# The small MLP's steps moved into the last slots of clustered attention, and the first batch's inputs taken ahead of the others

## The reference

```python
def first_block(z):                              # z = _layernorm(x) without weights
    u = _layernorm(z, ln1_g, ln1_b)
    q, k, v = (einsum('bsd,dhf->bshf', u, W) for W in (Wq, Wk, Wv))
    qb = softmax(einsum('bshf,hfn->bshn', q, Whq))      # cluster shares, 32 per head
    kb = softmax(einsum('bshf,hfn->bshn', k, Whk))
    logits = einsum('bqhf,bkhf->bhqk', q, k) / sqrt(DH) + 0.1 * einsum('bqhn,bkhn->bhqk', qb, kb)
    z = einsum('bshf,hfd->bsd', softmax(logits) @ v, Wo) + z           # clustered attention
    y = relu(_layernorm(z, ln2_g, ln2_b) @ W1 + b1) @ W2 + b2          # the small MLP, 512 wide
    return z + y
x = x + first_block(_layernorm(x))
x = x + two_local_layers(_layernorm(x))    # attention in windows of 64 tokens, and a gated MLP, twice
```

## Time and profile before

| | |
|---|---|
| median of 3 runs | 1464.22 us (1463.91 to 1464.61) |
| profiled execution, its own time | 1465.65 us |
| span of the profile | 1463.8 us |
| mean granted clock of PE | 0.962 |
| busy, share of the span | PE 87%, DVE 75%, ACT 68%, POOL 56% |
| instructions | 27861 |

### The profile page before, as it was taken

The page is one execution under the profiler, slowest core; times in us unless marked ns, Lnnn a source line. Parts: engine busy times, 40 slices in busy tenths (PEclk is TensorE's granted clock), DMA queues, the critical chain, the costliest instruction groups (busy, mean ns, idle before and its releaser), DMA issues.

```text
span 1463.8 us, 27861 instructions
## 1 busy us (share of the span) xinstructions
PE 1268.3 (87%) x9636; PEld 643.2 (44%) x9636; DVE 1090.7 (75%) x1943; ACT 998.3 (68%) x2313; POOL 822.2 (56%) x1005
## 2 busy tenths in 40 slices
PE   3378989998998988679589999998988999999898
PEld 1112222222222322157256666665534666666554
DVE  4778888888888877223489999995447999999644
ACT  4236766676666666577488999985337999999632
POOL 3666666667766640022577888870028888877200
PEclk9659999999999999989799999999999999999999
DMA  3523333343334330010111111110101111111001
GB/s 103 110 42 65 73 59 65 60 79 58 66 58 73 65 59 1 1 57 1 37 26 27 27 30 27 28 27 2 47 15 42 31 30 27 27 27 31 1 17 41
DMA packets 161120, 60.87 MB, mean 42 GB/s; under 512 B 139691, under 2 KB 152789, under 8 KB 160981
## 3 DMA queue, kind: packets, MB, share of 16 engines
q1 hardware_dynamic: 160980, 59.09, 19.1%
HBM read 8.60 MB, written 2.10 MB: 7 GB/s over the span
## 4 chain that ended last, share of the span: by engine, by line
PE 29%; ACT 11%; DVE 7%; issue 4%; POOL 2%; ACTq 0%; DVEq 0%; POOLq 0%
ACT la_s L1735 8%; PE la_ring L1360 6%; PE la_ring L1372 3%; PE la_s L1393 3%; PE la_pT L1467 3%; DVE la_prob L1624 2%; PE la_pT L1406 2%; PE la_m L1539 2%; PE la_ring L1455 1%; PE la_pT L1457 1%; PE la_s L1455 1%; PE la_s L1457 1%; ACT la_v_own L1777 1%; PE la_s L1385 1%; PE la_o L1422 1%
## 5 line engine op out<-in xcount | busy, mean ns | idle before, releaser
L618 DVE TENSOR_REDUCE row_max<-max_ps 128x2 f32<-128x1024 f32 x256 | 312.9, 1222 | 70.6 <-PE max_ps L430 69.2
L670 ACT ACTIVATE prob<-scores_ps 128x1024 f32<-128x1024 f32 x256 | 262.2, 1024 | 147.8 <-PE scores_ps L410 144.3
L1735 ACT ACTIVATE la_s<-la_s,la_bias,la_inv 128x128 f32<-128x128 f32 x512 | 223.4, 442 | 7.0 <-DVE la_bias L1612 7.0
L1886 POOL TENSOR_TENSOR la_turned<-la_raw,lw_rot 128x1024 f32<-128x1024 f32 x64 | 150.9, 2358 | 115.6 <-PE la_ring L1372 70.1
L1360 PE MATMUL la_ring<-lw_wqkv,la_hT 128*128 128x512 f32 x384 | 202.4, 638 | 15.3 <-DVE la_swapped L1587 6.7
L410 PE MATMUL scores_ps<-stack 128*128 128x512 f16 x512 | 155.7, 386 | 42.0 <-ACT prob L670 41.1
L1892 POOL TENSOR_TENSOR la_turned<-la_turned,la_swapped 128x1024 f32<-128x1024 f32 x64 | 150.7, 2355 | 5.0
L444 PE MATMUL heads_ps<-prob,v_pad 128*32 128x512 f32 x1024 | 137.2, 608 | 1.1 <-ACT prob L670 1.1
L430 PE MATMUL max_ps<-stack 24*128 24x512 f16 x512 | 102.5, 397 | 31.2 <-DVE row_max L618 18.5
L410 PEld LDWEIGHTS scores_ps<-stack 128*128 128x128 f16 x512 | 34.2, 97 | 208.7 <-ACT prob L670 161.3
L1587 DVE TENSOR_TENSOR la_swapped<-la_ring,lw_rot 128x256 f32<-128x256 f32 x256 | 90.8, 415 | 33.3 <-ACT la_raw L1746 23.8
(11 more groups left out here) (177 smaller groups left out, 2765.7 us busy)
## 6 DMA issues: line engine op xcount, KB each, us to landing
la_v_back<-la_v_own SPq DMA_DIRECT2D x112, 128.0 KB, 2.3
X<-in_x SPq DMA_DIRECT2D x8, 256.0 KB, 5.4
stack<-stack_tok SPq DMA_TRANSPOSE x128, 3.2
out<-X SPq DMA_DIRECT2D x8, 256.0 KB, 2.3
lw_wqkv<-in_wqkv SPq DMA_DIRECT2D x2, 768.0 KB, 4.8
stack<-shift_row SPq DMA_DIRECT2D x64, 2.0 KB
lw_rot<-in_rot SPq DMA_DIRECT2D x2, 512.0 KB, 6.5
lw_w<-in_fw SPq DMA_DIRECT2D x2, 341.0 KB
```

Of the source, the lines that this page charges most:

```text
L618: nc.vector.tensor_reduce(row_max[:, grp % 2, w // 2, :, w % 2], max_ps[:], AX.X, ALU.max).then_inc(max_made, 1)
L670: nc.scalar.activation(prob[:, c % 4, 2 * pr:2 * pr + 2, :], scores_ps[:], ACT.Exp, scale=1.0 / LOGIT_SCALE).then_inc(exp_made, 1)
L1735: ins = nc.scalar.activation(s_ps[:, place(h), :], s_ps[:, place(h), :], ACT.Exp, bias=bias[:, T % 2, h:h + 1], scale=inv[:, T % 4, h:h + ...
L1886: nc.gpsimd.tensor_tensor(spun, raw[:, T % 2].rearrange("p s (h f) -> p s h f", f=LD), rot[:, T % TPB, :, 0, :].unsqueeze(2).to_broadcast( ...
```

## The change

It has two parts. **The opening:** SP loads batch 0, the four arrays that the fold of the cluster weights needs, and six more that the first tile needs, ahead of the other seven batches; each group has its own semaphore. The statistics and scales are made for batch 0 first (`FIRST`), those of batches 1 to 3 behind it, and those of batches 4 to 7 on DVE right behind the cluster subtraction of tile 0. The scales of the other 28 tiles (`REST`) are made within tile 1's steps. For the first four tiles ACT, not POOL, scales the input and writes both leading parts (`leading_part`); DVE only writes the query's rest. `standardise` starts 24 slots later. **The small MLP:** `mlp_and_turn` is gone. Its steps stand in the slots of attention from slot 239 on, seven slots to a batch (`mlp_at`), and each engine does them after the rest of the slot. Its buffers lie in the half of `stack` that is free by then, its PSUM tiles in banks that attention no longer uses. Square root and reciprocal are replaced by an addition and a power on POOL. The input side of its layer norm is made as each batch is finished: DVE's four aggregates behind the statistics in slot `41 + 32b`, POOL's `invert_input` in slot `42 + 32b`, DVE's `input_shift` in slot `43 + 32b`. Three of the local layers' loads are issued behind the opening's loads.

```diff
+            load_input(0)
+            for dst, src in fold_loads:
+                sp.dma_start(dst, src).then_inc(fold_loaded, 16)
             for dst, src in loads:
                 sp.dma_start(dst, src).then_inc(w_loaded, 16)
+            for b in range(1, B):
+                load_input(b)
+            for dst, src in late_loads:
+                sp.dma_start(dst, src).then_inc(late_loaded, 16)
+            for dst, src in early_loads:
+                sp.dma_start(dst, src).then_inc(early_loaded, 16)
...
+            def leading_part(x, side):
+                act.wait_ge(cl_share_made[side], x + 1)
+                act.wait_ge(qkv_made, x + 1)
+                if x >= 1:
+                    act.wait_ge(stack_made[side, 0], 16 * x)
+                    act.wait_ge(stack_made[side, 1], 16 * x)
...
+                nc.scalar.activation(in_stack(side, 0, (0, NB)[side], NB, 2),
+                                     share.unsqueeze(3).to_broadcast([P, H // 2, 2, 2, NB]), ACT.Copy)
+                nc.scalar.activation(in_stack(side, 1, (0, DH)[side], DH, 2),
+                                     feat.unsqueeze(3).to_broadcast([P, H // 2, 2, 2, DH]), ACT.Copy
+                                     ).then_inc(hi_made[side], 1)
...
-                if 0 <= n - FIRST_SLOT - 4 < NT - TPB:
-                    standardise(n - FIRST_SLOT - 4 + TPB)
+                if 0 <= n - FIRST_SLOT - 28 < NT - TPB:
+                    standardise(n - FIRST_SLOT - 28 + TPB)
...
+                for x in range(TPB):
+                    if x == tile_at_step(n, 11):
+                        leading_part(x, 1)
+                    if x == tile_at_step(n, 12 if x == TPB - 1 else 17):
+                        leading_part(x, 0)
...
             def token_stats(x):
                 dve.wait_ge(proj_added, x + 1)
                 for t in range(x * TPB, (x + 1) * TPB):
-                    nc.vector.bn_stats(stats[:, t, :], Z[:, t, :])
+                    nc.vector.bn_stats(stats[:, t, :], Z[:, t, :]).then_inc(tok_stats_done, 1)
+                dve.wait_ge(tok_stats_done, (x + 1) * TPB)
+                for t in range(x * TPB, (x + 1) * TPB):
+                    nc.vector.bn_aggr(in_moments[:, t, :], stats[:, t, :]).then_inc(in_moments_done, 1)
+
+            def input_shift(b):
+                at = slice(b * TPB, (b + 1) * TPB)
+                dve.wait_ge(in_inv_done, b + 1)
+                nc.vector.scalar_tensor_tensor(out=in_shift[:, at], in0=in_moments[:, at, 0], scalar=-1.0,
+                                               in1=in_inv[:, at], op0=ALU.mult, op1=ALU.mult
+                                               ).then_inc(in_shift_done, 1)
...
+            def invert_input(b):
+                at = slice(b * TPB, (b + 1) * TPB)
+                pool.wait_ge(in_moments_done, (b + 1) * TPB)
+                nc.gpsimd.tensor_tensor(in_var[:, at], in_moments[:, at, 1], mlp_eps[:, 0], ALU.add
+                                        ).then_inc(in_var_done, 1)
+                pool.wait_ge(in_var_done, b + 1)
+                nc.gpsimd.tensor_tensor(in_inv[:, at], in_var[:, at], power[:], ALU.pow).then_inc(in_inv_done, 1)
...
+            def mlp_slot(n):
+                m, k = mlp_at(n)
+                if k == 0 and batch_or_none(m + 1) is not None:
+                    turn_input(m + 1)
+                if k == 0 and batch_or_none(m - 3) is not None:
+                    turn_output(m - 3)
+                if 1 <= k <= MC and batch_or_none(m) is not None:
+                    first_product(m, k - 1)
+                if k > MC and batch_or_none(m - 1) is not None:
+                    second_product(m - 1, k - MC - 1)
+
+            def both(n):
+                if n < LAST_SLOT:
+                    slot(n)
+                mlp_slot(n)
+
+            run(both)
```

More of the change, by code:

```diff
@@ new lines, in clustered_attention, with tiles, batch_or_none, mlp_at @@
+        w_made, out_turned, XT_made = sem("mlp_w_made"), sem("mlp_out_turned"), sem("mlp_XT_made")
+        def tiles(buf, b):
+            return buf[:, b * TPB:(b + 1) * TPB, :]
+        def batch_or_none(b):
+            return b if 0 <= b < B else None
+        def mlp_at(n):
+            return (n - MLP_SLOT) // MLP_STEPS - 1, (n - MLP_SLOT) % MLP_STEPS
+        def run(slot):
+            for n in range(FIRST_SLOT, MLP_SLOT + MLP_STEPS * (B + 4)):
+                slot(n)
+        def h_bank(b, c):
+            return max_ps[:, c % 2, :] if b < 3 or c < 2 else scores_ps[:, c % 2, :]
@@ L368, in share_of @@
             return cl[:, x % 2, side].rearrange("p (h n) -> p h n", n=NB)
-        def skipped(side):
-            return TPB if side == 0 else 0
+        REST = slice(TPB, NT)
+        FIRST = slice(0, TPB)
         @block.tensor
         def _(pe):
-            pe.wait_ge(w_loaded, 16 * len(loads))
+            pe.wait_ge(fold_loaded, 16 * len(fold_loads))
             for i in range(2):
@@ L503, in slot, with turn_input @@
                     fill_bench(use)
-            over_slots(slot)
+            def turn_input(b):
+                pe.wait_ge(y_made, b + 1)
+                if b == 0:
+                    bench_is_read(BENCH_LAST[2])
+                elif b in (3, 4):
+                    pe.wait_ge(added, b - 2)
+                else:
+                    pe.wait_ge(yT_made, b)
+                for i in range(TPB):
+                    mm = nc.tensor.transpose(bench_ps[:, 2, i * P:(i + 1) * P], y[:, b % 2, i, :], mlp_ident[:])
+                mm.then_inc(turned, 1)
@@ new lines, in second_product @@
+            def second_product(b, half):
+                pe.wait_ge(h_made, MC * (b + 1))
+                if b < 2:
+                    pe.wait_ge(yT_made, b + 3)
+                elif b == 2:
+                    bench_is_read(BENCH_LAST[0])
+                elif b == 3:
+                    pe.wait_ge(heads_moved, B * 4)
+                else:
+                    pe.wait_ge(added, b - 1)
+                for i in (2 * half, 2 * half + 1):
+                    for c in range(MC):
+                        mm = nc.tensor.matmul(o_bank(b)[:, i * D:(i + 1) * D],
+                                              hid[:, b % 2, c, i * P:(i + 1) * P], w2[:, c, :],
+                                              start=(c == 0), stop=(c == MC - 1))
+                mm.then_inc(o_filled, 1)
@@ L531, in _, with input_scale @@
+            def input_scale(part, tiles):
+                dve.wait_ge(dev1_done, part + 1)
+                nc.vector.reciprocal(R1[:, tiles], dev1[:, tiles]).then_inc(r1_done, 1)
+            input_stats(0)
+            input_variance(0, FIRST)
+            for T in range(TPB):
+                ins = nc.vector.tensor_scalar(Z[:, T, :], X[:, T, :], moments[:, T, 0:1], r0[:, T:T + 1],
                                               ALU.subtract, ALU.mult)
             ins.then_inc(first_z_made, 1)
-            dve.wait_ge(dev1_done, 1)
@@ L534, in _ @@
-            nc.vector.reciprocal(R1[:], dev1[:]).then_inc(r1_done, 1)
+            input_scale(0, FIRST)
+            for b in range(1, 4):
+                input_stats(b)
             def filled(step, x):
@@ new lines, in mlp_slot, with both @@
+            def mlp_slot(n):
+                m, k = mlp_at(n)
+                b = every(n - SLOTS - 10, SLOTS, B)
+                if b is not None:
+                    invert_input(b)
+                if k == 2 and batch_or_none(m - 1) is not None:
+                    add_base(m - 1)
+                if k == MLP_STEPS - 1 and batch_or_none(m - 1) is not None:
+                    invert_output(m - 1)
+            def both(n):
+                if n < LAST_SLOT:
+                    slot(n)
+                mlp_slot(n)
```

646 lines of the change are left out of this document (316 added, 330 removed).

## The result

| | before | changed |
|---|---|---|
| median | 1464.41 us (4 runs, 1463.91 to 1464.78) | 1481.86 us (4 runs, 1480.82 to 1483.46) |
| ratio | | 1.0115, interval 1.0102 to 1.0129 |
| profiled execution, its own time | 1465.65 | 1481.12 |
| span | 1463.8 | 1479.3 |
| mean granted clock of PE | 0.962 | 0.953 |

What follows compares the result with a forecast made beforehand. PE was taken as busy for most of the span, held up in the opening, at the attention-MLP seam and by engines waiting within slots. +4.1 + 18.9 - 14.0 = +9.0 gave 1473 us, forecast 1467 to 1479, wider range 1457 to 1484.

Steps and rivals of the forecast that it cites:

- wider 1457 to 1484: Range of the final time in us, leaving out two rivals' joint case and the far end of a third.
- rival C: In attention, each stall also costs PE's clock: up to 1.7 us, six times, +10, 1483; chance 0.13.
- opening: Start of the kernel to tile 3's landing: first row-maximum score at 74.9 against 70.80, costing 4.1 us.
- wait of the shift: In attention, DVE's input_shift waits for POOL's power in six batches: +18.9 us in all.
- small MLP in the slots: MLP steps in attention's last slots: last copy at 688.2 against 702.22, -14.0 us.
- local layers: After the small MLP: their own part stays and the wait for loads was hidden before too; 0.
- 3.1 per batch: Attention: PE's row-maximum matmul moves from 190.02 to 193.1 us behind DVE's wait, in six batches.
- at each of the six stalls: Attention: by the skill's idle-array rule, the clock falls to half rate behind every one of six 3.1 us stalls.
- Nobody runs ahead: Attention: work queued behind DVE's and PE's waits, and ACT's exponential, all wait too; 3.1 us per batch.
- rival A: Opening: ACT's middle not in the chain, cycle 9.1, tile 3 some 8 us earlier; 1461; chance 0.13.
- The sign named for a right forecast: Opening: the first row-maximum score on PE comes at about 75 us.

Runs made afterwards that it cites:

- e11: The changed kernel as it is, run again beside the filler-transpose kernels: 1481.61 us, ratio 1.0106.
- e4: The kernel before with only the aggregates, invert_input and input_shift added in the same slots, the small MLP staying apart: 1488.12 us, ratio 1.0162.
- e9: The changed kernel with 20 overwritten identity transposes on PE ahead of its last work before each of the six waits: 1474.76 us, ratio 1.0056.
- e1: The changed kernel with DVE's input_shift of each batch four slots later: 1454.34 us, ratio 0.9925.
- e5: The changed kernel with the shift four slots later and the query part of tiles 0 to 2 moved to tile 3's slots: 1447.03 us, ratio 0.9875.
- e6: The changed kernel with the shift four slots later and POOL's add_base one step of seven slots earlier: 1450.83 us, ratio 0.9904.
- e3: The changed kernel with a second, unused power on POOL ahead of the one DVE waits for: 1488.36 us, ratio 1.0159.
- e2: The changed kernel with DVE's input_shift one slot later: 1454.90 us, ratio 0.9932.
- e10: The changed kernel with 20 filler transposes on PE in each of six batches and the shift four slots later: 1471.96 us.

## Why the prediction was right, and where its terms were off

The direction and the main mechanism were right: slower, by DVE's wait on POOL's power in six of the eight batches. But 1481.86 is above the 1467 to 1479 of the forecast itself; it lies inside the wider 1457 to 1484, close to rival C's 1483, and what rival C describes is what happened. Part of the fit is luck: the opening came out 5.3 below its term and the MLP 6.9 above, so that two errors nearly cancel. Against the profiled spans (15.5 and 15.4 us more than before), term by term; the wait's term is the distance from exponential 0 to 237:

| term | forecast | changed kernel | second execution (e11) | |
|---|---|---|---|---|
| opening | +4.1 | -1.2 | -0.7 | sign wrong |
| wait of the shift | +18.9 | +25.2 | +24.7 | one part too large, one missing |
| small MLP in the slots | -14.0 | -7.1 | -9.5 | too large |
| local layers | 0 | -1.5 | +0.9 | differs between executions |

- **The wait.** The step "3.1 per batch" was a little high: 2.7 where the clock did not fall, in the changed kernel and in e4. POOL's power was 1.04 and its addition 0.20, as taken; POOL was done 0.3 earlier, and the shift took 0.23. 6 x 2.7 = 16.2 of the steps' 26.5. The term that was missing is the clock: the other 10.3. The forecast had it as rival C with chance 0.13 and "up to 1.7" a batch, +10; it was 1.6 to 2.9 in five batches of six. (the earlier trace rows is the window from 1108 on; PE's wait ahead of it, 2.42 us, ended at 1106.41.) e9 shows that it hangs on PE's pause and not on DVE's wait. The Trainium skill (TensorE: Matmul & The Clock Gate, Part 1) has the gate fall to half rate when the array sits idle. The changed kernel's rows around 192 agree; batch 1's equal pause (2.59, then 1.00) does not, so "at each of the six stalls" was too strong. Looking back, rival C deserved more than 0.13. "Nobody runs ahead", so that nothing is made good, did not hold to the letter: about 0.3 a batch is given back behind each wait, in every kernel that has them and not in e1.
- **The opening.** The form of the chain was right (e5: the middle stands in it; its removal gave cycles of 9.1 to 9.3, where rival A's sum was 9.1). The sizes were not. Tile 0's query transpose was issued at 33.2 and not at 35.7 (the first maximum came 0.5 earlier, DVE's statistics took 4.2, not 5.4, and other work ran beside them), and the cycles were 13.4 and 12.0 where I had 14.6 and 13.3. Three pieces of each cycle were summed too large. ACT's rows start each about 0.1 us before the one ahead has ended, so that the two leading parts and the middle lasted 6.3 in tile 2, where the durations add up to 7.1 (7.8 and 8.4 in tile 1); the rest and the issue took 0.9 to 1.0 in place of 1.2; and the landing 4.7 in place of 5.0. 2.5 + 1.2 + 1.3 = 5.0 of the 5.3 missed. The sign named for a right forecast, a first row-maximum score at about 75, did not come: it was at 69.64.
- **The MLP.** The slots up to exponential 253 were nearly right at full clock: 4.9 forecast, 5.4 in e1. From there to the last copy I had 73.8, e1 has 77.9. e6 shows 2.5 of that in the late sum on POOL: the forecast counted the power in the tail, but not what is queued behind it on POOL. 1.3 is a period of 8.13 between turns (674.00, 682.13 and 690.27 in the changed kernel) where I took 7.88. The changed kernel's remaining 2.4 lie in the slots, which took 7.8 up to exponential 253; the clock was at 0.50 there from 617 to 621, where e1 had it in full up to exponential 253 at 614.2. In the second execution the whole term is -9.5, e1's is -9.4.
- **The local layers** ended 1.5 us closer to the last copy (760.1 against 761.6 from there to the span's end), but 0.9 farther from it in the second execution of the same kernel (762.5). The clock falls twice between 1090 and 1113 in the kernel before, once as in the earlier trace rows, and once in the same stretch of the changed one (windows of 10 us at 0.83). So no part of the 1.5 can be put down to the change.

## What to carry to other kernels

A result that nobody needs for 100 us or more must not be computed by an instruction that waits at the head of a busy engine's queue: put the consumer a few slots behind its producer, and the same work is free (27 us here, for one number). When a stall is priced, add what PE's clock does behind the pause, and look for it in the durations of the next matmuls, not in the clock row of the page. And of a moved step, check each queue for what now stands behind it: the sum on POOL cost 2.5 us only because a power was written ahead of it.

## What the runs showed of the hardware that I had not expected

- Behind a PE pause of 2.6 us in a stretch with a busy PE the granted clock fell to 0.50 in most cases and not in all: in five of six waits of the changed kernel (the odd one was batch 1 in one execution and batch 5 in another), in one of six in an execution of e4, in six of six with longer pauses (e3, 3.58). Executions of e4 differ by 8 us, at mean granted clocks of 0.960 and 0.954. Shorter pauses can be followed by a fall too: one of 1.91 in e9, and one of 1.31 in e2 at 601.65 (0.50 from 604 to 606), where e1's equal pause at 600.08 was not. Nor was one of 2.27 in e10.
- 20 superfluous transposes in each pause made the changed kernel 6.9 us faster.
- POOL's power on 128x4 took 1.02 to 1.04 us, five times its addition of the same size (0.20).
